# Row 3 of the image windows loaded ahead of the last two image parts, and a re-cut opening

## What is computed

```python
# tokenizer: x and its four diagonal shifts by 4 pixels, 10 channels
concat = jnp.concatenate((x, lu, ru, ld, rd), axis=1)
normed = (concat - mean) * rsqrt(var + 1e-7)      # one mean, one variance for an image
normed = normed * gamma + beta
y = conv(normed, W, stride 8, kernel 8) + b       # 13 x 13 = 169 tokens of 128 channels
h = concat([cls_tok, y])                          # 170 tokens
# attention without a softmax: a 128 x 128 state for each image
n = layernorm(h); q, k, v = n @ Wq.T, n @ Wk.T, n @ Wv.T
for t in tokens:                                  # one after another
    S = S + 0.01 * outer over the batch (v_t, k_t);  out_t = S @ q_t
h = h + out
h = h + ffn(layernorm(h))                         # ffn passes its input on, plus a masked edit
```

## Time and profile before

| | |
|---|---|
| median of 3 runs | 217.07 us (217.06 to 217.54) |
| the profiled execution | 217.46 us, of which the span of the trace is 215.6 us |
| TensorE busy in the span | 196.3 us (91%) |
| VectorE, ScalarE, GpSimd busy | 152.3, 127.7, 154.5 us |
| moved by DMA | 25.90 MB |

### The profile page before, as it was taken

One profiled execution on the slowest core, in us unless ns is written; L12 is line 12 of the kernel. 1 busy time (PEld: TensorE's weight loads), 2 busy tenths in 40 slices (PEclk: granted clock), 3 DMA queues, 4 the chain that ended last, 5 costly groups with the idle time before them and its releaser, 6 DMA issues.

```text
span 215.6 us, 5028 instructions
## 1 busy us (share of the span) xinstructions
PE 196.3 (91%) x1548; PEld 166.9 (77%) x1548; DVE 152.3 (71%) x758; ACT 127.7 (59%) x306; POOL 154.5 (72%) x129
## 2 busy tenths in 40 slices
PE   0699999999999999999999999999999999999720
PEld 0488897886888889788888888899888888888610
DVE  3639694684486675678687597687687687699892
ACT  4215777884443375475756565665665574577982
POOL 1069908899990999969999949938999541455671
PEclk9999999999999999999999999999999999999975
DMA  5999992745022006153053432022012012100356
GB/s 140 388 420 422 422 413 112 217 185 181 0 58 111 2 3 194 30 175 88 3 153 109 125 93 49 5 50 49 11 41 52 16 36 52 28 22 5 80 118 152
DMA packets 17216, 25.90 MB, mean 120 GB/s; under 512 B 1719, under 2 KB 13693, under 8 KB 17062
## 3 DMA queue, kind: packets, MB, share of 16 engines
q1 hardware_dynamic: 16486, 25.41, 36.5%
q10 hardware_dynamic: 704, 0.17, 0.4%
HBM read 19.65 MB, written 5.92 MB: 119 GB/s over the span
## 4 chain that ended last, share of the span: by engine, by line
PE 52%; POOL 15%; DMA 10%; DVE 8%; issue 7%; SPq 4%; ACT 2%; POOLq 0%; DVEq 0%; ACTq 0%
PE conv L575 25%; DMA images<-x_rows 10%; PE vr_ps L623 10%; POOL scaled L469 7%; PE first_ps L633 6%; PE outs L650 6%; POOL rstd L1337 3%; PE turn L608 3%; POOL g_low L1327 2%; DVE state L1007 2%; DVE state L999 2%; SPq L488 1%; PE conv L583 1%; DVE images L1028 1%; POOL rstd L1353 1%
## 5 line engine op out<-in xcount | busy, mean ns | idle before, releaser
L575 PE MATMUL conv<-scaled,wt 128*128 128x256 f32 (+3 forms) x432 | 111.7, 375 | 7.3 <-DMA wt<-weight 6.9
L469 POOL TENSOR_TENSOR scaled<-rows,gam 128x832 f32<-128x832 f32 (+1 forms) x54 | 84.7, 1588 | 17.6 <-DMA rows<-x_windows 17.3
L575 PEld LDWEIGHTS conv<-scaled,wt 128*128 128x128 f32 x432 | 71.7, 193 | 15.3 <-DMA wt<-weight 6.9
L817 ACT ACTIVATE values<-vr_ps,rstd 128x256 f32<-128x256 f32 x76 | 36.0, 473 | 62.8 <-PE vr_ps L623 50.1
L1337 POOL TENSOR_TENSOR rstd<-var,powers 128x8 f32<-128x8 f32 (+2 forms) x20 | 30.3, 1517 | 27.0 <-DVE var L1019 26.9
L999 DVE TENSOR_TENSOR state<-first_ps,state 128x128 f32<-128x128 f32 x76 | 22.1, 291 | 27.6 <-PE first_ps L633 22.2
L825 ACT ACTIVATE images<-images,ln_shift,ln_gain 128x128 f32<-128x128 f32 x80 | 37.3, 489 | 1.5 <-DVE ln_shift L1076 0.7
L623 PE MATMUL vr_ps<-w_high,g_low 128*128 128x256 f32 x77 | 30.8, 400 | 0.8 <-ACT values L817 0.8
L1327 POOL TENSOR_TENSOR g_low<-g_t,g_high 128x512 fp32r<-128x512 f32 x21 | 26.8, 1274 | 4.6 <-ACT g_high L804 4.6
L988 DVE BATCH_NORM_STATS2 ln_stats<-images 128x6 f32<-128x128 f32 x85 | 23.6, 284 | 4.8 <-ACT images L811 4.7
L1007 DVE TENSOR_TENSOR state<-second_ps,state 128x128 f32<-128x128 f32 x76 | 21.5, 282 | 2.1
(11 more groups left out here) (201 smaller groups left out, 273.5 us busy)
## 6 DMA issues: line engine op xcount, KB each, us to landing
rows<-x_windows SPq DMA_DIRECT2D x12, 864.0 KB, 4.8
out<-images SPq DMA_DIRECT2D x40, 128.0 KB, 2.4
images<-x_rows SPq DMA_DIRECT2D x4, 832.0 KB, 14.9
images<-x_rows SPq DMA_DIRECT2D x1, 1040.0 KB, 15.9
images<-x_rows SPq DMA_DIRECT2D x1, 624.0 KB, 20.7
rows<-x_windows SPq DMA_DIRECT2D x1, 448.0 KB, 6.1
gam<-gamma SPq DMA_DIRECT2D x1, 422.5 KB, 6.8
bet<-beta SPq DMA_DIRECT2D x1, 422.5 KB, 9.0
```

Of the source, the lines that this page charges most:

```text
L469: return eng.tensor_tensor(scaled[:, s, at + skip:at + N], window[:, skip:N], gains.unsqueeze(2).to_broadcast([P, N - skip, B]), ALU.mult)
L575: last = pe.matmul(conv_ps[g % 2][:, at:at + n * B], held, scaled[:, s, a % RING:a % RING + n], start=first, stop=(g < EARLY and s >= TOP ...
L817: act.activation(values[:, t % VALUE_SLOTS].rearrange("p a e -> p (a e)"), vr_bank(t)[:, 0:2 * E], ACT.Identity, scale=rho_of(t)).then_inc ...
```

## The change

SP issues row 3 ahead of image parts 5 and 6. Row 3's slot holds the offsets for row 0, so SP first waits for row 0's eight scales. Row 0 is scaled by VectorE in two cuts, tokens 0 to 7 of the four shifts and then 8 to 12. VectorE also scales the first three tokens of row 1 (five scales of 192 elements), GpSimd waits for these and scales the other ten. TensorE gets four matmuls on zeros (`zero_products`) around the first item; two shifts of group 1 go between the table products of gamma and beta; group 4 is issued in another order (`conv_fifth`: first halves of the shifts, then second halves) with four items ahead of the image sums, five behind them and one behind `scale_rows`; two items of group 5 (`AHEAD`) follow in the opening. `FIRST` begins with 4 in place of 2, two of which are those issued ahead, so the rest of the table moves by two items. The subtraction of the tables on VectorE stands behind image part 0 in place of part 1.

```diff
--- before.py
+++ after.py
@@ -95,7 +95,8 @@
 LATE_ITEMS = [item for g in range(EARLY, GROUPS) for item in conv_items(g)]
 LATE_COST = [n for _, _, _, n in LATE_ITEMS]
 
-FIRST = (2, 2, 1, 1, 1, 1, 1, 1)
+AHEAD = 2
+FIRST = (4, 2, 1, 1, 1, 1, 1, 1)
 
 
 def late_item_step(i):
@@ -150,6 +151,7 @@
 ROW_4_TOKENS = {-7: (0, 5), -6: (5, 4), -4: (9, 4)}
 EARLY_TOKENS = TOKENS * EARLY
 CORNER = 3 * N
+SECOND = 2 * TOKENS
 
 
 def pool_scales(r, s):
@@ -317,6 +319,7 @@
         own_scales_ready = sem("own_scales_ready")
 
         scaled_first = sem("scaled_first")
+        scaled_second = sem("scaled_second")
         scaled_rows = sem("scaled_rows")
         scaled_by_scalar = sem("scaled_by_scalar")
         scaled_by_vector = sem("scaled_by_vector")
@@ -436,7 +439,7 @@
         def wait_scaled(eng, s, a, n):
             last = (a + n - 1) // N
             if a // N == 0:
-                eng.wait_ge(scaled_first, s + 1)
+                eng.wait_ge(scaled_first, s + 1 if a < TOKENS else TOP + 1 + s + 1)
             if a + n - 1 == CORNER:
                 eng.wait_ge(corner_scaled, s + 1)
                 last -= 1
@@ -444,6 +447,8 @@
                 eng.wait_ge(scaled_by_scalar, BY_SCALAR.index((last, s)) + 1)
             elif (last, s) in BY_VECTOR:
                 eng.wait_ge(scaled_by_vector, 1)
+            elif 0 < last and a + n <= SECOND:
+                eng.wait_ge(scaled_second, s + 1)
             elif last > 0:
                 eng.wait_ge(scaled_rows, pool_scales(last, s))
 
@@ -457,17 +462,17 @@
             at = (t % PER_GROUP) * E
             return buf[t // PER_GROUP % slots][:, at:at + E]
 
-        def scale_shift(eng, r, s):
+        def scale_shift(eng, r, s, first=0, stop=N):
             offsets = (r if s < 3 else r - 1) % ROW_SLOTS
             right = N + (s - 1) % 2
             window = rows[:, r % ROW_SLOTS, 0:N] if s == 0 else rows[:, offsets, right:right + N]
-            skip = 1 if r * N == CORNER else 0
-            gains = gam_first[:, s] if r == 0 else gam[:, s, r * N + skip:r * N + N]
+            skip = 1 if r * N == CORNER else first
+            gains = gam_first[:, s, skip:stop] if r == 0 else gam[:, s, r * N + skip:r * N + stop]
             if (r, s) == (N - 1, BOTTOM):
                 gains = bottom[:, E:E + N]
             at = r % 2 * N
-            return eng.tensor_tensor(scaled[:, s, at + skip:at + N], window[:, skip:N],
-                                     gains.unsqueeze(2).to_broadcast([P, N - skip, B]), ALU.mult)
+            return eng.tensor_tensor(scaled[:, s, at + skip:at + stop], window[:, skip:stop],
+                                     gains.unsqueeze(2).to_broadcast([P, stop - skip, B]), ALU.mult)
 
         block = ctx.enter_context(nc.Block())
 
@@ -481,6 +486,8 @@
                         sp.wait_ge(scaled_by_vector, 1)
                     if r - 3 >= CORNER // N:
                         sp.wait_ge(corner_scaled, SHIFTS)
+                if r == ROW_SLOTS:
+                    sp.wait_ge(scaled_second, SHIFTS)
                 sp.dma_start(rows[:, r % ROW_SLOTS], x_windows[:, r]).then_inc(row_in[r % ROW_SLOTS], 16)
 
             def load_images(i):
@@ -513,11 +520,10 @@
             load_images(2)
             load_images(3)
             load_images(4)
+            sp.wait_ge(scaled_first, 2 * (TOP + 1))
+            load_row(3)
             load_images(5)
             load_images(6)
-
-            sp.wait_ge(scaled_first, TOP + 1)
-            load_row(3)
             load_row(4)
             for blk in range(2):
                 count = P if blk == 0 else PATCHES - P
@@ -588,9 +594,14 @@
                     if a <= item[1] < z:
                         conv(item)
 
+            def conv_fifth(a, z):
+                items = conv_items(EARLY - 1)
+                for item in (items[0::2] + items[1::2])[a:z]:
+                    conv(item)
+
             def late_conv(t, half):
 
-                share = [i for i, st in enumerate(ITEM_STEPS) if st == t]
+                share = [i for i, st in enumerate(ITEM_STEPS) if st == t and i >= AHEAD]
                 mid = (len(share) + 1) // 2
                 for i in share[:mid] if half == 0 else share[mid:]:
                     conv(LATE_ITEMS[i])
@@ -703,15 +714,28 @@
                 reads(LAST)
                 reads(LAST + 1)
 
+            def zero_products(count):
+                for _ in range(count):
+                    pe.matmul(vr_ps[:, 0:PER_GROUP * E], zeros[:], zeros[:].unsqueeze(1).to_broadcast([P, PER_GROUP, E]),
+                              start=True, stop=True, skip_group_check=True)
+
+            pe.wait_ge(zeros_ready, 1)
+            zero_products(3)
             pe.wait_ge(weight_in, 16)
-            conv_shifts(0, 0, SHIFTS)
-            pe.wait_ge(gamma_in, 16)
-            pe.wait_ge(beta_in, 16)
-            for kind, table in enumerate((bet, gam)):
+            conv_shifts(0, 0, 1)
+            zero_products(1)
+            conv_shifts(0, 1, SHIFTS)
+            def table_columns(kind, table):
                 for i in range(SHIFTS):
                     last = pe.matmul(turn_ps[:, kind * PATCHES:kind * PATCHES + PATCHES], wt[:, i], table[:, i], start=(i == 0),
                                      stop=(i == SHIFTS - 1), skip_group_check=True)
-            last.then_inc(columns_done, 1)
+                return last
+
+            pe.wait_ge(gamma_in, 16)
+            table_columns(1, gam)
+            conv_shifts(1, 0, 2)
+            pe.wait_ge(beta_in, 16)
+            table_columns(0, bet).then_inc(columns_done, 1)
             pe.wait_ge(small_in, 16)
             pe.wait_ge(centered, 3)
             pe.matmul(out_ps[:, 0:E], wk_c[:], wq_c[:], start=True, stop=True, skip_group_check=True)
@@ -724,7 +748,7 @@
                 for kind in range(2):
                     last = pe.transpose(ps[0:count, kind * E:kind * E + E], columns[:, kind, blk * P:blk * P + count], small[:, IDENT])
                 last.then_inc(tables_done, 1)
-            conv_shifts(1, 0, SHIFTS)
+            conv_shifts(1, 2, SHIFTS)
             pe.wait_ge(cls_t_ready, 1)
             pe.wait_ge(w_vr_ready, 2)
             pe.matmul(vr_ps[:, 0:2 * E], cls_t[:], w_vr[:], start=True, stop=True).then_inc(vr_done, 1)
@@ -744,24 +768,26 @@
             pe.matmul(first_ps[:, 0:E], values[:, VALUE_SLOTS - 1, 0], values[:, VALUE_SLOTS - 1, 1], start=False,
                       stop=True, skip_group_check=True).then_inc(cls_state_done, 1)
             conv_shifts(3, 0, SHIFTS)
+            conv_fifth(0, 4)
             pe.wait_ge(sums_ready, 2)
             pe.wait_ge(w_low_ready, 1)
             pe.wait_ge(scalar_sums_ready, 3)
             pe.matmul(out_ps[:, 2 * E:2 * E + 2], small[:, SAME], sums[:], start=True, stop=False, skip_group_check=True)
             pe.matmul(out_ps[:, 2 * E:2 * E + 2], small[:, SAME], scalar_sums[:], start=False, stop=True,
                       skip_group_check=True).then_inc(image_sums_done, 1)
-            conv_shifts(EARLY - 1, 0, 2)
+            conv_fifth(4, 9)
             pe.wait_ge(scale_cols_ready, 1)
             pe.matmul(out_ps[:, 0:B], scale_cols[:], small[:, IDENT, 0:B], start=True,
                       stop=True).then_inc(scale_rows_done, 1)
-            conv_shifts(EARLY - 1, 2, 4)
+            conv_fifth(9, 10)
+            for item in LATE_ITEMS[0:AHEAD]:
+                conv(item)
             pe.wait_ge(own_scales_ready, 1)
             pe.wait_ge(early_rows_ready, 1)
             early(0)
             pe.wait_ge(state_ready, 1)
             early(1)
             early(2)
-            conv_shifts(EARLY - 1, 4, SHIFTS)
             pe.matmul(out_ps[:, 0:E], cls_t[:], state[:, STATE_SLOTS - 1, 1], start=True,
                       stop=True).then_inc(out_done, 1)
             for t in range(START, TAIL):
@@ -1223,7 +1249,13 @@
                     dve.wait_ge(first_right_in, 16)
                 if s == TOP:
                     dve.wait_ge(first_offsets_in, 16)
-                scale_shift(dve, 0, s).then_inc(scaled_first, 1)
+                scale_shift(dve, 0, s, 0, TOKENS).then_inc(scaled_first, 1)
+            for s in range(TOP + 1):
+                scale_shift(dve, 0, s, TOKENS).then_inc(scaled_first, 1)
+            dve.wait_ge(gamma_in, 16)
+            dve.wait_ge(row_in[1], 16)
+            for s in range(SHIFTS):
+                scale_shift(dve, 1, s, 0, SECOND - N).then_inc(scaled_second, 1)
 
             dve.wait_ge(small_in, 16)
             for i, w in enumerate((WQ, WK)):
@@ -1258,16 +1290,17 @@
                         else:
                             part = part.rearrange("p r (g q) -> p r g q", q=HALF)[:, :, 0:S // HALF:S // HALF - 1]
                         last_stats = dve.bn_stats(stats[:, 2 * j:2 * j + 2].rearrange("p a b -> p (a b)"), part)
+                if i == 0:
+                    for blk, ps in enumerate((turn_ps, second_ps)):
+                        m = P if blk == 0 else PATCHES - P
```

(12 more changed lines are left out.)

## The result

The changed kernel takes 219.31 us in the median of 14 executions (217.26 to 220.69), the kernel before 217.60 (217.06 to 217.89). The ratio of the means is 1.0071 with a 95% interval of 1.0045 to 1.0097: slower by 0.7%, where 217.0 was forecast and the range ended at 218.9. Ratios here are of means, and this one leaves out the longest execution, 220.69, which is over 1.5% above the shortest; with it, it is 1.0076.

A forecast was written before the change was run, and what follows sets the result against it. TensorE, busy 91% of the span, was taken as the bound, with the image sums' arrival set by the image transfer. 2.18 - 0.88 - 0.88 - 0.49 = -0.07 gave 217.39, less 0.39 for the runs' median: 217.0 us, range 216.2 to 218.9.

The forecast's parts named there:

- the gap's price: TensorE stands idle ahead of the image sums for about 2.4 us; the sum held no term for its clock.
- Its fall: TensorE's clock falls in the new gap ahead of the image sums: +1.8 us, so 218.8; chance 0.25.
- less than about 1.6 us, this case is out: The clock's fall is ruled out if TensorE's gap ahead of the image sums is less than about 1.6 us.
- The price of 1.8: TensorE behind the gap: at least 3.57 us of matmuls at the low clock, half of it lost, +1.8 us.
- the 0.39 taken off for the runs' median: Whole kernel: 217.39 against the profiled execution; the median of the runs was 0.39 below it, so 217.0.
- image sums on TensorE: The last image parts land later and the image sums follow: +2.18 us.
- sums to the first step: TensorE behind the sums: ten items before the first step become eight, -0.88 us.
- first step to the last products: The steps have two items less, -0.88 us, and the stall of 0.49 near 91 goes, -0.49 us.
- Row 3 ahead of parts 5 and 6: In the full DMA queue, row 3 issued first makes both last image parts land 2.18 us later.
- What the early row buys: GpSimd runs one scale of row 3 early; the power and other three scales move 2.18 later, to 41.86; nothing charged.
- Stalls: In the steps, the second stall, 0.49 us near 91, should go; the first, 0.63 near 51, stays.
- The opening at nothing: VectorE's cuts and the zero matmuls delay nothing the sums wait for; GpSimd ends row 1 at 20.15, not 20.59.

## Why the prediction was wrong

**The step that failed is the gap's price, which the sum puts at nothing.** The sum has no term for TensorE's clock. Its fall was a rival with a chance of 0.25 and a price of 1.8 us, at 218.8, and the forecast took the case in which the clock holds. The fall is what most executions did: 11 of 14 took 219.0 and more. With the clock held by zeros the same kernel takes 217.56, so the missing term measured 1.7 us. The trace had shown the clock fall 1.6 us after the last matmul, behind a thin tail, and the gap was put at 2.4 us. That number spoke for the fall, and the run told of by the page was allowed to weigh against it. The Trainium skill, "TensorE: Matmul & The Clock Gate", Part 1, Seeing it yourself, has 5.2 us from the last matmul to the fall; here a gap of 2.17 us sufficed (in the profile where it fell). The measurement decides. The condition "less than about 1.6 us, this case is out" did not hold up either: with a gap of 1.54 us in the profile 3 of 10 executions took the higher times.

**The price of 1.8 fits the middle group, in part by luck, and is too small for the upper.** It was half of the 3.57 us for which matmuls were seen at the low clock in the opening, and no row said that a fall in the gap would last as long. The middle group lies 1.6 us above the lower one (219.3 against 217.7). In the one profiled fall the clock stayed low for 6.8 us and cost 3.1.

**The base was low as well.** The rival's 218.8 is 217.0 + 1.8, and the median of 219.31 lies above the range because the lower group is at 217.7 and not at 217.0. Of that, 0.3 is the sum (below). The rest is the 0.39 taken off for the runs' median: it came from three executions with a median of 217.07, and 14 executions of the kernel before have 217.60.

**The sum** is judged on the profile with the clock held, 217.68 against 217.39 foreseen, 0.29 off:

| term | forecast | measured |
|---|---|---|
| image sums on TensorE | +2.18 | +2.33 (33.34 to 35.67) |
| sums to the first step | -0.88 | -0.80 (6.19 to 5.39 us) |
| first step to the last products: two items less, one stall less | -1.37 | -1.23 (164.58 to 163.35 us) |
| sum | -0.07 | +0.30 |

- *Row 3 ahead of parts 5 and 6*: right. The last part is 2.34 us later, and with the loads in the old order the kernel gains 2.23.
- *What the early row buys*: right. One scale runs early, the other three only behind the power, and `g_low` starts at 41.99 without a wait. That this is the very time worked out is chance: ScalarE had its input ready at 41.91, and GpSimd, busy with the scales until then, was the last. That the row could be of use shows only in the kernel in which ScalarE, GpSimd and TensorE take it up.
- *Stalls*: right. The second is gone, the first stays at 0.63.
- *The opening at nothing*: right for time, but GpSimd ended row 1 at 20.61, no earlier than before: its 640-element scales took 1.23 us each, not 1.19, and it started at 14.48, 1.61 behind the row, which VectorE read from 12.87 on.
- *The gap*: 2.77 us in place of 2.4. Of the 0.36, 0.15 is the later sums and some 0.2 the opening. That sum put four items of group 1 between the tables without saying where their room comes from: it is the clock, as the items of group 0 ran at 0.46 us and not at 0.89.
- *"Opens nearly as much as it fills"* was the right sentence, but the gap isn't free.

**What stays open.** Which gap lets the clock fall in a given execution: the counts below give shares, no limit. The middle group has no profile of its own; that it is a shorter stay at the low clock is suggested by the mean clocks (0.971 to 0.977 against 0.963 to 0.971), and not shown. The length of a wait alone does not decide: ahead of the first weights TensorE stood for 1.61 us behind the zeros in the changed kernel's profile, and the two items from 7.02 still took 0.49 us each.

## What to carry to other kernels

A wait of TensorE of some 2 us could cost more here than its own length: price it with the clock, in the trace's own numbers, and either fill it with real work or hold the clock with matmuls on zeros. A transfer put ahead in a full queue delayed what stood behind it by its own length (2.2 us here), so it pays only if everything that can use it has been moved ahead as well. When work is moved forward in a table, look again at the short operations that share an engine with it: one power behind two scales was a gap of 2.15 us.

## What the runs showed of the hardware

That the clock falls in gaps so short, and only in part of the executions, was not expected. The longest wait of TensorE between 14 us and the last steps, as the one profile of each kernel has it in its brackets (a stall of 0.63 or 2.15 us between an item's end by its distance and the next start stands there as 0.37 or 1.89), and the executions in the upper groups of times:

| kernel | wait | executions with the higher times |
|---|---|---|
| row 3 used, no stall | 0.23 us | 0 of 4 |
| before | 0.37 | 0 of 14, and 0 of 47 beside the other kernels |
| changed kernel, three on zeros | 0.37 | 0 of 12 |
| loads alone in the new order, two on zeros | 0.38 | 0 of 4 |
| loads in the old order | 0.47 | 0 of 4 |
| loads in the old order, no early shifts | 1.08 (at 16.70) | 0 of 4 |
| one matmul on zeros | 1.54 | 3 of 10 |
| row 3 used, stall in the steps | 1.89 | 7 of 12 |
| loads alone in the new order | 2.21 | 2 of 4 |
| changed kernel | 2.77, and 2.17 | 11 of 14, and 2 of 2 |

Matmuls on zeros whose result nobody reads hold the clock as real ones do (0 of 12 and 0 of 4). They seem to raise it early, too: with them the items from 9.06 us ran at the full rate, without them those from 9.34 at half. No run took the zeros of the opening out alone, so this rests on the comparison of the kernels with the re-cut opening and those without.
